# Attention bias added by half-row identity products from a halved table, two normalisations and a residual moved from VectorE to GpSimd, and the bias writes shared 3 to 5

## The reference

```python
# attention, 16 heads of 8 channels
x  = x + layernorm(attention(layernorm(x)))
#   scores = q @ k.T / sqrt(8) + bias,  bias[h, i, j] = rel_bias[clip(i - j + 128, 0, 256), h]
#   softmax over j, times v, times W_out, plus b_out
# feed-forward, hidden width 512, ternary weights with a scale for each output
x  = x + layernorm(ffn(layernorm(x)))
#   h = silu(x @ w1 * s1) * (x @ w2 * s2)
#   h = gelu(h @ h1 * h1s); h = gelu(h @ h2 * h2s); y = h @ w3 * w3s
```

## Time and profile before

| | |
|---|---|
| median of 3 runs | 291.94 us (289.52, 291.94, 294.78) |
| the profiled execution's own time | 286.88 us |
| its span | 285.0 us |
| TensorE, busy share of the span | 92% |
| VectorE | 75% |
| ScalarE | 74% |
| GpSimd | 36% |
| granted TensorE clock | 0.9 or more of full speed until the last of 40 slices |

### The profile page before, as it was taken

The page is one execution under the profiler, slowest core; times in us unless marked ns, Lnnn a source line. Parts: engine busy times, 40 slices in busy tenths (PEclk is TensorE's granted clock), DMA queues, the critical chain, the costliest instruction groups (busy, mean ns, idle before and its releaser), DMA issues.

```text
span 285.0 us, 5125 instructions
## 1 busy us (share of the span) xinstructions
PE 261.2 (92%) x1847; PEld 175.5 (62%) x1847; DVE 213.7 (75%) x443; ACT 212.1 (74%) x322; POOL 102.8 (36%) x107
## 2 busy tenths in 40 slices
PE   7899989999899998999998997788999999999980
PEld 7656645565555554555654654447888888888860
DVE  4676977989789889888898898859654853673576
ACT  2677777987878888887878878567469976896750
POOL 6716000101702603934986957017740302400111
PEclk9999999999999999999999999999999999999996
DMA  6979504522221355370322000000000000010012
GB/s 155 329 244 146 193 7 153 183 61 77 75 75 41 91 195 186 95 222 23 93 77 56 25 1 1 2 2 2 0 2 0 0 0 2 0 37 0 2 39 78
DMA packets 21356, 21.17 MB, mean 74 GB/s; under 512 B 3664, under 2 KB 18768, under 8 KB 21072
## 3 DMA queue, kind: packets, MB, share of 16 engines
q1 hardware_dynamic: 20464, 20.53, 24.8%
q10 hardware_dynamic: 864, 0.27, 0.5%
HBM read 14.90 MB, written 5.64 MB: 72 GB/s over the span
## 4 chain that ended last, share of the span: by engine, by line
PE 61%; DVE 20%; ACT 11%; issue 5%; POOL 1%; DMA 1%; ACTq 0%; POOLq 0%; DVEq 0%
PE place L1521 10%; PE place L1522 10%; PE place L1299 8%; DVE mx L703 7%; PE pv L1351 7%; ACT ring L1046 6%; PE place L1291 5%; PE place L1325 3%; DVE place L710 3%; ACT place L1053 2%; PE place L1250 2%; DVE stats L627 2%; PE misc L1229 2%; PE pv L1522 2%; PE misc L1362 2%
## 5 line engine op out<-in xcount | busy, mean ns | idle before, releaser
L703 DVE TENSOR_REDUCE mx<-place 128x4 f32<-128x1024 f32 x64 | 78.3, 1223 | 16.6 <-PE place L1299 15.2
L525 POOL TENSOR_TENSOR rstd<-mv,mhalf 128x2 f32<-128x2 f32 (+1 forms) x26 | 21.0, 806 | 143.2 <-DVE mv L635 143.1
L1046 ACT ACTIVATE ring<-place 128x1024 f32<-128x1024 f32 x64 | 65.5, 1028 | 1.1 <-PE place L1336 0.2
L1053 ACT COPY place<-raw 128x1024 f32<-128x1024 f32 x43 | 43.8, 1020 | 14.2 <-DVE mx L703 14.0
L1299 PE MATMUL place<-room,identr 128*128 128x512 f32 x128 | 46.9, 448 | 0.0
L1521 PE MATMUL place<-room,w_hi 128*128 128x512 f32 (+1 forms) x116 | 44.6, 387 | 0.7 <-DVE room L855 0.7
L1522 PE MATMUL place<-room,w_hi 128*128 128x512 f32 (+1 forms) x116 | 44.0, 382 | 0.0
L1325 PE MATMUL place<-room 33*128 33x256 f32 x256 | 31.9, 328 | 4.4 <-DVE place L710 2.9
L1351 PE MATMUL pv<-ring,vx 128*9 128x256 f32 x512 | 33.6, 380 | 0.7 <-ACT ring L1046 0.7
L855 DVE TENSOR_TENSOR room<-ring,room 128x512 fp32r<-128x512 f32 x32 | 21.3, 689 | 17.1 <-ACT room L1151 17.1
L1291 PE MATMUL place<-room 33*128 33x256 f32 x256 | 28.5, 299 | 4.1 <-ACT ring L1046 4.1
(11 more groups left out here) (146 smaller groups left out, 422.7 us busy)
## 6 DMA issues: line engine op xcount, KB each, us to landing
raw<-ext SPq DMA_DIRECT2D x8, 384.0 KB, 6.6
room<-q_parts SPq DMA_DIRECT2D x48, 64.0 KB
room<-k_parts SPq DMA_DIRECT2D x48, 64.0 KB
w_lo<-h SPq DMA_DIRECT2D x2, 1024.0 KB, 5.6
q_parts<-w_hi SPq DMA_DIRECT2D x4, 256.0 KB, 3.0
k_parts<-w_hi SPq DMA_DIRECT2D x2, 512.0 KB, 3.7
xs<-x SPq DMA_DIRECT2D x3, 256.0 KB, 5.6
w_lo<-w SPq DMA_DIRECT2D x3, 256.0 KB, 2.9
```

The source lines that it names most:

```text
L525: nc.gpsimd.tensor_tensor(rstd[:, at:at + width], mv[:, at:at + width, 1], mhalf[:, 0:width], ALU.pow).then_inc(rstd_set, 1)
L703: nc.vector.tensor_reduce(mx[:, s // RPAIRS, :, :, s % RPAIRS].rearrange("p i k -> p k i"), max_tile(b * PAIRS + s)[:, :, :].rearrange("p ...
L1046: nc.scalar.activation(probs[:, s % PRING, :, :, :].rearrange("p k j n -> p (k j n)"), score_tile(b * PAIRS + s)[:, :, :].rearrange("p k n ...
L1053: nc.scalar.copy(score_tile(i)[:, :, :].rearrange("p k (j n) -> p k j n", j=2), pair_windows(raw[:, :, :], i % PAIRS)).then_inc(bias_set, 1)
```

## The change

The table for the max pass is held for 64 positions instead of 128. Partitions 0 to 63 hold the first head of a pair and 64 to 127 the second, each row 448 columns long, loaded straight from memory in this form (`load_halves`, into a part of `w_lo` that is free then). A product of 64 rows with an identity of 64 columns, shifted within a strip of zeros (`ident_wide`), fills the upper or the lower 64 outputs and adds zero to the others. So a pair takes four products of 64 rows and 512 columns, two heads times two blocks, where it took two of 128 rows. The products of the two heads lie in different halves of the array and write different banks. The exact table `raw` is still needed for `write_bias`, and its eight loads move behind the first stores of q and k: four before and four after the rows of batch 1 and the first row of maxima.

The normalisation of y, its addition to x, and the second normalisation go to GpSimd, for all batches but the last. VectorE takes the moments of the sum (`x1_moments`) after pair 6, where it did the second normalisation. VectorE writes the bias of pairs 2, 5 and 7, ScalarE that of the other five. In the last batch VectorE writes the bias of pair 3 before `weigh(B - 2, 0)` and that of pair 5 after `weigh(B - 2, 1)`. The pieces of the weight split go to other batches and another order, two a batch in batches 1 to 5 and one in 6. TensorE gets four products with a blank tile after pair 7 of batches 1 and 6; there were two, in batch 6. `score_bias` becomes eight half-row products in the same way.

```diff
-BY_DVE = (2, 5)
+BY_DVE = (2, 5, 7)
...
-        table_hi = room[:, hi_at:lo_at].rearrange("p (h c) -> p h c", h=H)
+        raw_halves = w_lo[:, 2 * PAIRS * P:2 * PAIRS * P + PAIRS * TWIN].rearrange("p (s c) -> p s c", s=PAIRS)
+        table_hi = room[:, hi_at:lo_at].rearrange("p (s c) -> p s c", s=PAIRS)
+        ident_wide = room[:, ident_at:ident_at + 3 * HP]
...
-        SPLIT_AT = ((), (0,), (1,), (2, 3), (4, 5, 6), (7, 8, 9), (10,), ())
+        SPLIT_AT = ((), (0, 1), (2, 3), (8, 9), (4, 5), (6, 7), (10,), ())
...
+        def load_halves(eng, s):
+            eng.dma_start(raw_halves[:, s, :],
+                          bass.AP(tensor=ext.tensor, offset=2 * s * EXT,
+                                  ap=[[EXT, 2], [1, HP], [1, TWIN]])).then_inc(table_in[s], 16)
...
             store_parts(1)
+            for s in range(PAIRS // 2):
+                load_table(sp, s)
             sp.wait_ge(parts_out[1], PARTS_OUT)
             row_dmas(1, 0, PAIRS, second_rows_in)
+            send_mrow(sp, 0, 0)
+            for s in range(PAIRS // 2, PAIRS):
+                load_table(sp, s)
             load_x(4)
-            send_mrow(sp, 0, 0)
             store_parts(2)
...
+            def residual(b):                      # GpSimd
+                inv_std(b * 2 + NU + 1, TPB)
+                pool.wait_ge(rstd_set, b * 2 + NU + 1)
+                for t in range(TPB):
+                    last = pool_normalize(y[:, t, :], y[:, t, :], t)
+                last.then_inc(y_norm, 1)
+                pool.wait_ge(y_norm, b + 1)
+                xb = xs[:, TPB * b:TPB * b + TPB, :]
+                nc.gpsimd.tensor_tensor(xb, xb, y[:, :, :], ALU.add).then_inc(x1_set, 1)
...
-                    inv_std((b - 1) * 2 + NU + 1, TPB)
-                    inv_std((b - 1) * 2 + NU + 2, TPB)
-                    pool.wait_ge(z_set, b)
+                    residual(b - 1)
+                    second_norm(b - 1)
...
-                        if s == 5:
-                            residual(b - 1)
                         if s == 6:
...
-                            second_norm(b - 1)
+                            x1_moments(b - 1)
...
             first = (B - 1) * PAIRS
             write_bias(first + 2)
+            write_bias(first + 3)
             weigh(B - 2, 0)
-            write_bias(first + 3)
             write_bias(first + 4)
+            weigh(B - 2, 1)
             write_bias(first + 5)
-            weigh(B - 2, 1)
             largest_low()
             write_bias(first + 7)
             attn_moments(B - 2)
             any_low()
-            residual(B - 2)
             z_low(B - 3)
-            second_norm(B - 2)
+            x1_moments(B - 2)
...
+            def bias_product(tile, table, s, block, half):
+                at = half * HP
+                return mm(tile[:, half, :], ident_wide[at:at + HP, HP - block * HP:3 * HP - block * HP],
+                          windows(table[at:at + HP, s, :], block * HP, P, 2, S), start=False, stop=True,
+                          skip_group_check=True)
...
-                for half in range(2):
-                    last = mm(max_tile(b * PAIRS + s)[:, half, :], identr[:, :],
-                              windows(table_hi[:, 2 * s + half, :], 0, P, 2, S),
-                              start=False, stop=True, skip_group_check=True)
+                for block in range(2):
+                    for half in range(2):
+                        last = bias_product(max_tile(b * PAIRS + s), table_hi, s, block, half)
...
-                        if b + 2 == B:
+                        if b in (1, B - 2):
                             pe.wait_ge(oT_set, (b + 1) * GROUPS - 1)
-                            stream(pv, blank, blank, 2)
+                            stream(pv, blank, blank, 4)
```

More of the change, by code:

```diff
@@ L23 @@
 EXT = WIN + P - 1
+HP = P // 2
+TWIN = WIN + HP
 CH = 512
@@ L99, in build @@
         ident = sb("ident", [P, P])
-        identr = sb("identr", [P, P], F32R)
         wq_sb = sb("wq_sb", [P, D])
@@ L243, in build @@
         rows_set = sem("rows_set")
+        table_in = [sem(f"table_in{s}") for s in range(PAIRS)]
         table_hi_pool = sem("table_hi_pool")
@@ L337, in build @@
         WPIECES = WCOLS // WPIECE
-        SPLIT_AT = ((), (0,), (1,), (2, 3), (4, 5, 6), (7, 8, 9), (10,), ())
+        SPLIT_AT = ((), (0, 1), (2, 3), (8, 9), (4, 5), (6, 7), (10,), ())
+        SPLIT_ORDER = [piece for pieces in SPLIT_AT for piece in pieces]
         def wait_gate_low(eng, c, k):
@@ L531, in table_high @@
             def table_high(s):
[L532 to L534 removed]
+                pool.wait_ge(table_in[s], 16)
+                nc.gpsimd.tensor_copy(table_hi[:, s, :], raw_halves[:, s, :]).then_inc(table_hi_pool, 1)
             x_inv_std(0)
@@ L695, in _ @@
             nc.vector.tensor_scalar(bq_sb[:, 0:1], bq_sb[:, 0:1], scale, None, ALU.mult).then_inc(bq_scaled, 1)
-            nc.vector.tensor_copy(identr[:, :], ident[:, :]).then_inc(identr_set, 1)
+            dve.wait_ge(blank_set, 1)
+            nc.vector.tensor_copy(ident_wide[:, 0:2 * HP], blank[:, :]).then_inc(identr_set, 1)
+            nc.vector.tensor_copy(ident_wide[:, 2 * HP:3 * HP], blank[:, 0:HP]).then_inc(identr_set, 1)
+            dve.wait_ge(identr_set, 1)
+            for half in range(2):
+                at = half * HP
+                nc.vector.tensor_copy(ident_wide[at:at + HP, HP:2 * HP],
+                                      ident[at:at + HP, at:at + HP]).then_inc(identr_set, 1)
             x_moments(2)
@@ L745, in residual, with x1_moments @@
                 nc.vector.tensor_tensor(xb, xb, y[:, :, :], ALU.add).then_inc(x1_set, 1)
+            def x1_moments(b):
                 dve.wait_ge(x1_set, b + 1)
@@ L902, in _ @@
             residual(B - 1)
+            x1_moments(B - 1)
             layer_low(1, 0, (2, 3))
@@ L1333, in score_bias @@
                 pe.wait_ge(table_lo_set, low + 1)
-                for half in range(2):
-                    for part in (table_hi[:, 2 * s + half, :], table_lo[:, 2 * low + half, :]):
-                        last = mm(score_tile(b * PAIRS + s)[:, half, :], identr[:, :], windows(part, 0, P, 2, S),
-                                  start=False, stop=True, skip_group_check=True)
+                for table, at in ((table_hi, s), (table_lo, low)):
+                    for block in range(2):
+                        for half in range(2):
+                            last = bias_product(score_tile(b * PAIRS + s), table, at, block, half)
                 last.then_inc(st_ready, 1)
```

75 lines of the change are left out of this document (48 added, 27 removed).

## The result

The changed kernel takes 316.16 us (median of 4 runs, 314.29 to 317.78) where the kernel before takes 290.73: a ratio of 1.090, 95% interval [1.079, 1.101], 9% slower. The forecast was 283 us and faster. Ratios leave out executions that ran over 1.5% above the fastest of their kernel.

The account below looks back on a forecast made before the run. TensorE was taken as the bound by a little (19.3 us a batch), VectorE 1 us behind. Seven loops 7.7, start 0.5 and end 0.5 sum to 8.7 us: 283 us by ratio 0.970, range 275 to 290.

Parts of the forecast that it names:

- the one on the loads: Start and batch 0: smaller max-pass tables come early, exact tables follow; cost taken at nothing, 3 us as far end.
- The rival that loads come late: GpSimd's chain or moved loads late: 1 us a loop or 3 us at the start lost, 286 to 289 us; chance 0.05.
- Half-row products side by side: TensorE, batch loops: products in different array halves overlap, 0.77 us against 0.89 and 1.00, gaining 1.4 us a batch.
- The rival with 302 us: Half-row products don't run side by side: TensorE needs 21.4 us a batch, loop 1.9 us or more longer; chance 0.06.
- Loops of 18.9 us: Batch loops: 17.9 us for the busiest engines plus 1.0 us for bursts, a gain of 1.1 us a loop.
- TensorE and VectorE meet at 17.9: Batch loops: TensorE falls from 19.3 and VectorE from 18.3 us, both to 17.9 us a batch.
- GpSimd's chain: Power, two normalisations at 0.5 us, addition 0.75 us, hand-overs: first part 2.8 us, at worst 4.1; second part 1.9 us.
- The cover: VectorE's own work between `attn_moments` and `x1_moments`, 3.7 us, or two pairs of TensorE, 4.6 us, hides GpSimd's first part.
- The end: Last batch and after: 1.0 us gained up to the projection, 1.2 lost on GpSimd's exposed chain, gate products sooner; net 0.5 gained.
- the 1.0 counted up to the projection: Last batch: VectorE writes pair 3's bias during TensorE's transposes for `weigh`, and `score_bias` gets shorter; 1.0 us gained.
- The ring at the start: Batch 0 max passes: `row_lows`, `keep_rows`, `take` keep a 2.47 us period for six pairs; only 0.5 us gained after.
- GpSimd slows VectorE: Rival: VectorE's bias copies slow by a factor of 1.2, loop 19.7 us, time 288.8 us; chance 0.05.

Follow-up runs that it names:

- the loads alone: Kernel before plus eight idle loads of 224 KB with outer dimension 2, nothing else of the change: ratio 1.105 [1.097, 1.113], 31.6 us more in the medians.
- wide loads: Changed kernel with each half-row table load cut in two, one per head, outermost dimension 64 instead of 2: ratio 0.963 [0.953, 0.973], span 283.2 us.
- two kernels of this kind: Changed kernel with loads of 64, plus either batch 6's residual and second normalisation back on VectorE (0.986) or VectorE's biases cut to pairs 2 and 5 (0.990).
- the last norms on VectorE: Changed kernel with loads of 64, batch 6's residual and second normalisation back on VectorE: ratio 0.986 [0.979, 0.993]; again on another chip 0.958 [0.952, 0.963].
- idle loads in four shapes: Kernel before plus 224 KB loads nobody needs, outer dimension 2, 64, 16 or 4: ratio 1.105 for 2, then 305.1 (median), 307.5 and 317.2 us.
- the half rows: Changed kernel with loads of 64, normalisations, residual and third bias put back as before: ratio 0.964 [0.956, 0.973]; again on another chip 0.967 [0.963, 0.972].
- the blanks: Changed kernel, narrow loads kept, plus 100 blank products on TensorE while it waits for the first probabilities: ratio 1.095 [1.090, 1.100], span down 3.0 us.
- four blanks in a shorter wait: Kernel with loads of 64 and batch 6's norms on VectorE, plus four blank products after the last batch's second scores: 0.959 [0.954, 0.963], against 0.958 without.

## Why the prediction was wrong

The step that failed is the one on the loads: "the tables for the max pass fall from 384 to 224 KB each and come early", "Taken at nothing, with 3 us as the far end". I costed transfers by their bytes. The access pattern stood in the diff, with its 2 in front, and the loads before had 128 there. It cost 29.2 us before the first exponential, and by the clock that fell in the wait 3.6 us more in batch 0. With the outer dimension of 64 both are gone from the profile; the loads alone, in the kernel before, cost 10.5%. The Trainium skill, DMA: Bandwidth & Descriptors, section "Why a DMA increments its semaphore by 16 and not by 1", states the rule: the number of engines is the largest up to 16 that divides the slowest dimension of both access patterns. The share of 0.13 agrees with it, and the shares of 0.39, 0.67 and 1.09, which have wide loads between the others, rise with the outer dimension as it would have it. No rival of mine had the mechanism. The rival that loads come late had the place right and 3 us for its price; it was 29.

The rest of the forecast did not come true either, though the ratio of 0.963 with wide loads looks like the 0.970 forecast. That likeness is luck: there the kernel before had the lower clock. Profile against profile, where 8.7 us of gain were forecast, 1.8 came (283.2 against 285.0 us). Where both have the higher clock, the ratios of two kernels of this kind are 0.986 and 0.990. The terms of the sum, forecast and measured in that profile: start 0.5 gained, 0.2 lost; the seven loops 7.7 gained, 4.7 gained (6.1 in the profile with the last norms on VectorE, whose clock stayed up there); last batch and end 0.5 gained, 2.7 lost. The kernel before falls under a mean clock of 0.975 more often than the kernels with wide loads, in 22 of 25 runs on the three chips against 6 of 35. Why, no run here tests, and none of those 22 has a profile. The kernels with idle loads in four shapes do show where the clock falls once it does: in batches 2, 6 and 7 the last three of the table take 1.5, 1.5 and 4 us more than the kernel before in its profile, 7 us in all, which is near the difference between its runs at the two clocks.

Step by step otherwise:

- *Half-row products side by side.* Right. 0.80 us for scores to next group, forecast 0.77, so 1.2 us a batch (4 x 0.09 + 4 x 0.20) instead of 1.4. The rival with 302 us, products one behind the other, did not happen; that the time came out beyond it has another cause. (Its 15 us were added to the profiled 286.88; on the median of 291.94, as in the other rivals, they give 307.)
- *Loops of 18.9 us.* Right in the mean only, and partly by luck: batches 1 to 6 take 113.1 us, 18.9 each, against 19.8 before. The gain of 1.1 us in every loop was 0.6 to 0.8 in batches 2 to 4, which take 19.9, 19.4 and 19.4 us, and 1.0 to 1.5 in batches 1, 5 and 6.
- *TensorE and VectorE meet at 17.9.* Wrong as a reason. VectorE had room, since giving a bias back to ScalarE changed none of the loops 2 to 6. The gain of batches 2 to 4 is that of the half rows (19.8, 19.4 and 19.4 us with those only, and 19.9, 19.4 and 19.4 with all). The moved work shows in batch 1 (18.6 against 19.3), in batch 5 (18.5 against 19.3) and in batch 6 (17.5 against 18.2), all at a clock of 1.00 in the changed kernel and in the second profile of the half rows. As the third bias does nothing in batches 5 and 6, there it is the normalisations. Why there and not in 2 to 4 stays open.
- *GpSimd's chain.* The size was off: a normalisation takes 0.80 us, above my upper bound of 0.75, taken as 0.5; the addition 0.73, as forecast. The cover held in the loops: no wait of VectorE for it is in the trace from 87 to 200 us.
- *The end.* "Net 0.5 us gained, between 1.5 gained and 1 lost": 2.8 us are lost behind the last exponential, and the 1.0 counted up to the projection came to 0.1 with loads of 64 and to a loss of 1.2 in the changed kernel, whose clock fell there. With the last norms back on VectorE 1.6 to 2.0 of the 2.8 return (99.0 to 99.4 us). The term was mis-sized, 0.3 us for each of four normalisations, and TensorE's wait of 2.1 us has no slack behind it. What makes up the remaining 0.8 to 1.2 us wasn't tested; the two profiles of the half rows have 98.5 and 99.2 against 98.2 before.
- *The ring at the start.* Right: with wide loads `row_lows` still follow each other every 2.47 us, at 15.30, 17.77 and 20.25 us in the half-row kernel. The 0.5 us forecast there did not come: the first exponential of the kernels with wide loads stands between 0.2 us earlier and 1.2 us later than before.
- *GpSimd slows VectorE.* It did not: VectorE's bias copies take 1.216 to 1.228 us in the changed kernel as well.

## What to carry to other kernels

Read the access pattern of a new or changed load before its bytes: with 2, 4 and 16 as its outermost dimension the same bytes kept ever more DMA engines busy, and the narrow transfers held up those behind them in their queue, wide ones too. Put the partitions, or a multiple of 16, outermost, at the price of two transfers if it must be. Where two engines look equally full, move a piece of work between them and see whether the loop answers, before more is moved. And look at the clock of both kernels before believing a ratio: here it alone makes 2 to 3% of difference.

## What the hardware showed beside this

The granted clock of TensorE turned one late load into two costs. From 42 to 46 us TensorE was busy for 0.8 of 4 us; from 45 to 50 us the clock averaged 0.58, and from 50 us on it stood at 0.5 (1.2 GHz of 2.4), through the idle stretch to 62 us and up to 70. Batch 0 took 3.9 us more than with the blanks. There the clock averaged 0.50 from 50 to 55 us, 0.99 in the next five and 1.00 from 60 to 80 us. Waits are not all there is to it: four blanks in a shorter wait gave nothing to be measured, and the same kernel fell to 0.5 in its last batch in one run and not in another.

In the last batch the cost can be read off directly, over all profiles. It takes 12.4 to 12.8 us where its mean clock is 1.00, 13.7 to 14.1 at 0.88, and 16.9 to 17.1 at 0.70.

A GpSimd `tensor_scalar` with two pointer scalars takes 0.80 us for 128 columns, where VectorE takes 0.34. One with an immediate takes 1.50 for 512 columns, so four times the columns take 1.9 times as long; the two differ in more than their columns.
